# Attention and experts on one core: reciprocals through memory, bf16 parts for roots and maxima, normalisation in pieces, slots written out

## The reference, cut to what matters

```python
# x (8, 64, 128, 64), txt (8, 32, 64); all float32
h = tok(x, W)                        # patches of 16, stride 8, rfft, linear: (8, 1024, 64)
h = concatenate([h, txt], axis=1)    # (8, 1056, 64)
# layernorm(h) = (h - mean) / sqrt(var + 1e-5), over the 64 features
q, k, v = heads(layernorm(h) @ w_qkv.T)                 # 4 heads of 16
a = softmax(q @ k.T * 0.25) @ v
h = h + a.reshape(8, 1056, 64) @ w_proj.T + b_proj
n = layernorm(h)
p = softmax(n @ gate_w + gate_b)     # 8 experts, weights of the two largest kept in cw
h = h + sum_e cw[e] * (gelu(n @ W1[e] + b1[e]) @ W2[e] + b2[e])
```

## Time and profile before

| | |
|---|---|
| median of 3 runs | 997.62 us (996.91 to 1000.64) |
| the profiled execution | 1001.97 us, span 1000.2 us |
| busy in the span | PE 899.0 (90%), DVE 573.0 (57%), ACT 494.4 (49%), POOL 138.7 (14%) |
| mean granted TensorE clock | 0.922 |
| DMA | 64.58 MB in 55864 packets |

### The profile page before, as it was taken

How to read it: one execution, slowest core, us unless ns; L and a number is a source line. 1 busy time by engine, 2 the same in 40 slices (tenths; PEclk the granted TensorE clock), 3 DMA queues, 4 the chain that set the end, 5 groups by cost and what they waited for, 6 DMA issues and landing times. The chain is left out here.

```text
span 1000.2 us, 17890 instructions
## 1 busy us (share of the span) xinstructions
PE 899.0 (90%) x5900; PEld 374.9 (37%) x5900; DVE 573.0 (57%) x1201; ACT 494.4 (49%) x1189; POOL 138.7 (14%) x148
## 2 busy tenths in 40 slices
PE   5665899999999989999999999999965989899996
PEld 5241322433342343343243334333412535354443
DVE  4025565578874557876557887788230553636331
ACT  0020254466664536665446676666533454555552
POOL 0010100011010011101001101001000344444443
PEclk9965589899999988999989999999876999999998
DMA  8329351027551005536002305100006655382731
GB/s 153 57 47 163 62 62 31 3 35 119 97 69 44 2 4 67 117 67 110 2 1 30 40 2 68 44 3 1 1 5 141 120 126 117 80 184 52 155 78 22
DMA packets 55864, 64.58 MB, mean 65 GB/s; under 512 B 23893, under 2 KB 41825, under 8 KB 55777
## 3 DMA queue, kind: packets, MB, share of 16 engines
q1 hardware_dynamic: 55777, 63.46, 35.5%
HBM read 36.73 MB, written 2.43 MB: 39 GB/s over the span
## 5 line engine op out<-in xcount | busy, mean ns | idle before, releaser
L887 DVE TENSOR_REDUCE max_parts<-bank 128x1 f32<-128x512 f32 x512 | 329.6, 685 | 137.4 <-PE bank L1075 134.5
L811 ACT ACTIVATE probs<-bank 128x384 f32<-128x384 f32 (+1 forms) x768 | 313.4, 466 | 191.1 <-PE bank L1038 189.6
L1038 PE MATMUL bank<-q_stack,k_stack 99*128 99x384 bf16 (+1 forms) x768 | 229.9, 329 | 4.9 <-ACT probs L811 4.2
L1075 PE MATMUL bank<-k_stack,q_stack 96*128 96x512 bf16 x512 | 208.4, 409 | 17.2 <-DMA k_stack<-part 13.2
L1016 PE MATMUL bank<-probs,v_tiles 128*32 128x384 f32 (+1 forms) x1536 | 160.2, 490 | 5.4 <-ACT heads_out L796 5.0
L1038 PEld LDWEIGHTS bank<-q_stack,k_stack 99*128 99x128 bf16 x768 | 72.2, 99 | 196.1 <-ACT probs L811 146.1
L1285 ACT ACTIVATE hid<-bank,biases 128x352 f32<-128x352 f32 x192 | 96.0, 552 | 84.8 <-PE bank L1329 84.7
L1304 DVE SCALAR_TENSOR_TENSOR prod<-bank,biases,cwb 128x352 f32<-128x352 f32 x96 | 55.8, 582 | 120.1 <-PE bank L1317 103.0
L1329 PE MATMUL bank<-x,w 128*128 128x352 bf16 (+1 forms) x576 | 105.2, 320 | 6.3 <-DMA x<-part 6.3
L1317 PE MATMUL bank<-hid,w_sb 128*64 128x352 f32 x384 | 79.2, 491 | 7.7 <-DVE prod L1304 4.0
L1052 PE MATMUL bank<-x,tok_m 128*64 128x512 f32 x256 | 68.5, 634 | 9.4 <-DMA text_in<-in_txt 8.0
(11 more groups left out here) (146 smaller groups left out, 704.2 us busy)
## 6 DMA issues: line engine op xcount, KB each, us to landing
cwb<-gates_by_expert SPq DMA_DIRECT2D x16, 1056.0 KB, 12.1
x<-in_x SPq DMA_DIRECT2D x64, 256.0 KB, 6.9
q_stack<-part SPq DMA_DIRECT2D x48, 132.0 KB, 6.1
k_stack<-part SPq DMA_DIRECT2D x48, 132.0 KB, 6.6
x<-part SPq DMA_DIRECT2D x32, 132.0 KB, 2.5
h_res<-h_new SPq DMA_DIRECT2D x4, 528.0 KB, 3.0
h_all<-h_res SPq DMA_DIRECT2D x4, 528.0 KB, 3.1
h<-h_all SPq DMA_DIRECT2D x8, 264.0 KB, 3.2
```

The source lines that it names most:

```text
L811: nc.scalar.activation(probs[:, group % 3, h, 0:n], src, ACT.Exp, scale=SCALE).then_inc(exp_done, 1)
L887: nc.vector.tensor_reduce(max_parts[:, c, H * j + h, i % 2:i % 2 + 1], src[:, :], AX.X, ALU.max)\
L1038: last = nc.tensor.matmul(bank[:, 0:n], ks[par][0:ROWS + 3, h, P * kt:P * kt + P], qs[par][0:ROWS + 3, h, QC[qc]], start=True, stop=True)
L1075: last = nc.tensor.matmul(bank[:, :], queries(h, j), ks[par][0:ROWS, h, HALF * (i % 2):HALF * (i % 2) + HALF], start=True, stop=True)
```

## The change

- The reciprocals go from SBUF to a table in memory, `recip_rows`, and from there come back over 16 partitions per head in four transfers (`spread` 1 and 2). The three matmuls L1147 and ACT's three copies are gone; POOL multiplies at units 24, 26, 28 (`normalise`), PE projects at 27, 30, 33.
- `stack` is issued in two halves, at units 3 and 26 (7 and 30 in slot 0).
- The maxima are negated once, split into three bf16 parts on 128 partitions by DVE before the turning matmul; that matmul is bf16, and one copy on DVE ends it.
- The token variances stand at units 74, 75, 76, three tiles in each; the roots at 76 to 80, each Newton step in a unit of its own, and a split into three bf16 parts at 80 (four operations more). The spread of the roots is three bf16 matmuls for each f32 one, at units 86, 88, 90. Beside the experts the same helpers run without being spread out.
- `embed` starts two units later, `project` stands at 36, 39, 42 and 92, 94, 97.
- The loop over slots 1 to 4 is written out.

```diff
-AT_FINISH = [17, 20, 23, 26, 29, 32]
-AT_EMBED = [list(range(32, 47, 2)), list(range(48, 63, 2))]
-AT_TOKENISE = [AT_EMBED[0][-1], AT_EMBED[1][-1], 65, 68, 71, 74, 77, 80, 82, 84]
-AT_PROJECT = {"odd": [34, 37, 40], "even": [89, 92, 95]}
+AT_NORMALISE = [24, 26, 28]
+AT_FINISH = [27, 30, 33]
+AT_STACK = [3, 26]
+AT_EMBED = [list(range(34, 49, 2)), list(range(50, 65, 2))]
+AT_VARY = [74, 75, 76]
+AT_ROOT = [77, 78, 79, 80]
+AT_TOKENISE = [AT_EMBED[0][-1], AT_EMBED[1][-1], 66, 68, 70, 72, AT_VARY[-1], 86, 88, 90]
+AT_PROJECT = {"odd": [36, 39, 42], "even": [92, 94, 97]}
...
-                for i in range(2):
+                for i in range(3):
                     order.append(("spread", i, b - 1, 1 - par, q, g))
-            if u == (AT_FIRST["project"][-1] + 1 if "first" in stages else 0):
-                for i in range(2):
-                    if "following" in stages:
-                        order.append(("stack", i, b + 1, 1 - par, q + 1, g))
+            for i in range(2):
+                if "following" in stages and u == AT_STACK[i] + (AT_FIRST["project"][-1] if "first" in stages else 0):
+                    order.append(("stack", i, b + 1, 1 - par, q + 1, g))
...
-            with eng.Fori(0, 2) as q:
+            for q in range(2):
...
+        def split_roots(dve, done, n):
+            t, y = root_work[:, 1, :], roots[:, :]
+            nc.vector.tensor_copy(root_part[:, 0, :], y).then_inc(done, 1)
+            nc.vector.tensor_tensor(t, y, root_part[:, 0, :], ALU.subtract).then_inc(done, 1)
+            nc.vector.tensor_copy(root_part[:, 1, :], t).then_inc(done, 1)
+            return nc.vector.tensor_tensor(root_part[:, 2, :], t, root_part[:, 1, :], ALU.subtract)
...
-                for bp in range(2):
-                    last = nc.tensor.matmul(bank[D * bp:D * bp + D, tokens.start - WIDE * i:tokens.stop - WIDE * i],
-                                            roots[0:n, 2 * t + bp:2 * t + bp + 1].broadcast_to([n, D]),
-                                            ident[0:n, 0:n], start=True, stop=True)
+                for part in range(3):
+                    for bp in range(2):
+                        col = 2 * t + bp
+                        last = nc.tensor.matmul(bank[D * bp:D * bp + D, tokens.start - WIDE * i:tokens.stop - WIDE * i],
+                                                root_part[0:n, part, col:col + 1].broadcast_to([n, D]),
+                                                ident_half[0:n, 0:n], start=(part == 0), stop=(part == 2),
+                                                skip_group_check=True)
...
+                    elif (stage, i) == ("spread", 1):
                         sp.wait_ge(recip_done, t + 1)
-                        sp.dma_start(recip_rows[DH:P:32, :], den[:, :]).then_inc(recip_moved, 16)
+                        sp.dma_start(recip_rows, den[:, :]).then_inc(recip_moved, 16)
+                    elif stage == "spread":
+                        sp.wait_ge(recip_moved, 16 * (t + 1))
+                        for h in range(H):
+                            sp.dma_start(recip[32 * h:32 * h + DH, :], recip_rows[h:h + 1, :].broadcast_to([DH, L]))\
+                              .then_inc(recip_spread, 16)
...
-                    elif stage == "finish" and i % 2 == 0:
-                        freed(pool, i, g)
+                    elif stage == "normalise":
+                        pool.wait_ge(recip_spread, 16 * H * (t + 1))
+                        pool.wait_ge(side_free, g)
...
-                    elif stage == "finish" and i % 2 == 0:
-                        bank = full(act, i, g)
-                        nc.scalar.activation(recip[:, chunk[i // 2]], bank[:, 0:CH], ACT.Copy).then_inc(side_free, 1)
...
+                            dve.wait_ge(neg_step, step + 1)
+                            nc.vector.tensor_copy(neg_part[:, kinds, :, 0, :], negm[:, kinds, :, :]).then_inc(neg_step, 1)
+                            dve.wait_ge(neg_step, step + 2)
+                            nc.vector.tensor_tensor(neg_rest[:, kinds, :, :], negm[:, kinds, :, :],
+                                                    neg_part[:, kinds, :, 0, :], ALU.subtract).then_inc(neg_step, 1)
+                            dve.wait_ge(neg_step, step + 3)
+                            nc.vector.tensor_copy(neg_part[:, kinds, :, 1, :], neg_rest[:, kinds, :, :]).then_inc(neg_step, 1)
+                            dve.wait_ge(neg_step, step + 4)
+                            nc.vector.tensor_tensor(neg_part[:, kinds, :, 2, :], neg_rest[:, kinds, :, :],
+                                                    neg_part[:, kinds, :, 1, :], ALU.subtract).then_inc(neg_max, 1)
...
-                        nc.vector.tensor_copy(m_high[:, :], src).then_inc(shift_step, 1)
-                        stt(out=m_rest[:, :], in0=m_high[:, :], scalar=take_high, in1=src, op0=ALU.mult, op1=ALU.add)\
...
+                        nc.vector.tensor_copy(m_part[:, :], max_bank[place][0:3 * QR, 0:P]).then_inc(max_done, 1)
...
-                        last = nc.tensor.matmul(bank[0:3 * QR, 0:P], negm[:, c // 2, :, :, :].rearrange("p k n h -> p (k n h)"), ident, start=True,
-                                                stop=(c < NCH - 1), skip_group_check=True)
+                        last = nc.tensor.matmul(bank[0:3 * QR, 0:P],
+                                                neg_part[:, c // 2, :, :, :].rearrange("p k n h -> p (k n h)"),
+                                                ident_half[:, :], start=True, stop=(c < NCH - 1), skip_group_check=True)
...
-                        if i % 2 == 0:
-                            last = nc.tensor.matmul(bank[:, 0:CH], den_sel, recip_rows[:, chunk[c]], start=True, stop=True)
```

More of the change, by code:

```diff
@@ L355, in run_phase1 @@
                     side("embed", (i, j), None, None, 0, 0)
+                for j in range(2 if i == 6 else 0):
+                    side("vary", j, None, None, 0, 0)
                 side("tokenise", i, None, None, 0, 0)
+                for j in range(4 if i == 6 else 0):
+                    side("root", 1 + j, None, None, 0, 0)
             for i in range(USES["project"]):
@@ L431, in build, with token_variances @@
         wide = [slice(WIDE * i, min(WIDE * i + WIDE, L)) for i in range(NCH)]
-        def token_variances(bank, squares):
-            for t, tokens in enumerate(NORM_TILES):
+        def token_variances(bank, squares, part):
+            for t in range(3 * part, 3 * part + 3):
+                tokens = NORM_TILES[t]
                 rows = slice(0, tokens.stop - tokens.start)
@@ L438, in token_variances, with first_guess @@
             return last
-        def inverse_roots(dve, y, work, bank, done, n):
-            v, t = work[:, 0, :], work[:, 1, :]
+        def first_guess(dve, bank, done, n):
+            v, t = root_work[:, 0, :], root_work[:, 1, :]
             base = ROOT_STEPS * n
@@ L550, in norm_vector @@
                 dve.wait_ge(norm_full, NORM_FILLS * p + ROOTS + 1)
-                inverse_roots(dve, roots[:, :], root_work, norm_bank(p, ROOTS), roots2_step, p).then_inc(norm_read, 1)
+                first_guess(dve, norm_bank(p, ROOTS), roots2_step, p)
+                for k in range(3):
+                    newton_step(dve, k, roots2_step, p)
+                split_roots(dve, roots2_step, p).then_inc(norm_read, 1)
             elif name == "scale":
@@ L616, in norm_tensor @@
             elif name == "roots":
-                last = token_variances(bank, sq)
+                for part in range(3):
+                    last = token_variances(bank, sq, part)
             elif name == "scale":
-                last = spread_roots(bank, roots, i)
+                last = spread_roots(bank, i)
             elif name == "gates":
@@ L898, in side @@
                             dve.wait_ge(max_done, at + 1)
-                            for n in range(3):
-                                last = nc.vector.tensor_reduce(negm[:, c // 2, 0:nt, n, :], parts[:, 0:nt, :, :], AX.X,
-                                                               ALU.max, negate=True)
+                            step = 4 * (NCH * t + c)
+                            kinds = slice(0, 1) if c < NCH - 1 else slice(1, 3)
+                            last = nc.vector.tensor_reduce(negm[:, kinds.start, 0:nt, :], parts[:, 0:nt, :, :], AX.X,
+                                                           ALU.max, negate=True)
                             if c == NCH - 1:
@@ L1138, in side @@
                         elif i == 6:
[L1139 removed]
+                            last = token_variances(bank, sq, 2)
                         else:
[L1141 removed]
+                            last = spread_roots(bank, i - 7)
                     elif stage == "finish":
[L1143 to L1150 removed]
+                        pe.wait_ge(on_ready, NCH * t + i + 1)
+                        last = nc.tensor.matmul(bank[rows, 0:CH], projT[:, :], on[:, chunk[i]], start=True, stop=True)
```

154 lines of the change are left out of this document (80 added, 74 removed).

## The result

The changed kernel takes **995.66 us** (median of 20 executions, 984.8 to 1010.91) against 997.58 (20 executions, 995.29 to 1002.41) of the kernel before on the same chip. The ratio of the comparison is 0.9927, 95% interval 0.9905 to 0.9948; it leaves out the 7 of the changed kernel's 20 executions that lie over 1.5% above its fastest and have a mean granted clock of 0.900 to 0.912, while the means over all 20 executions of each are 997.4 and 999.0. Forecast were 978 and a range of 957 to 993.

The account below looks back on a forecast made before the run. PE was taken to bound the kernel, busy for 90% of the span. Gains of 36.9 us less 17 for the stack in halves gave -19.9 from 997.62: 978 us, range 957 to 993.

Parts of the forecast that it names:

- Term 4: Shift of the negated maxima: cheaper bf16 turning matmul, DVE's longer chain mostly covered by two units of maxima; -3.3 us.
- Terms 1 and 2: Reciprocals through memory: spreading matmuls gone from the slots, -11.6 us; shorter chain after slot 7, -5.0 us.
- Term 3: Loop's way back from slot 2 to 3: writing it out saves idle issue time and low clock, -6.6 us.
- Term 8: Stack in halves lands late in slots 1, 3, 5; ACT and PE stop at `project`, low clock follows: +17 us.
- Terms 5 to 7: In order: bf16 root fills, -3 us; variances and roots in pieces, -8; small ends beside experts and before slot 0, +0.6.
- Rival A: No wait at `project`, as the stack's second half lands before unit 36: 961 us, chance 0.20.
- rival D: Root-fill loads serialise and PE waits for the shifts: 986 to 999 us, chance 0.08.
- Rival B: Clock not given back: three low stretches stay, stalls bring their own, slot 3 falls low: 988 us, chance 0.12.
- a sum of the slots less than 10 us shorter: Sign over the slots: if their sum falls by less than 10 us, a bound other than PE has taken over.

Follow-up runs that it names:

- experiment 7: Changed kernel with both halves of the stack issued at unit 3: 1019.01 us, ratio 1.0161 to the kernel before.
- experiment 3: Kernel before with only the loop over slots 1 to 4 written out: 993.87 us, ratio 0.9926.
- experiment 11: Kernel of experiment 9 with the stack issued in two halves, at units 3 and 26: 989.06 us, ratio 0.9897.
- experiment 6: Changed kernel with odd-slot `project` at units 44, 47, 50 and the maxima in f32 as before: 973.39 us, ratio 0.9738.
- experiment 2: Changed kernel with odd-slot `project` at units 44, 47, 50 in place of 36, 39, 42: 977.89 us, ratio 0.9791.
- second run: The changed kernel, unaltered, timed and profiled again beside the kernel before: 999.0 us, ratio 0.9954.
- experiment 4: Changed kernel with the 18 variance matmuls in one burst at unit 76: 991.21 us, ratio 0.9893.
- experiment 12: Kernel of experiment 8 with the 18 variance matmuls in one burst at unit 76: 973.16 us, ratio 0.9718.
- experiment 5: Changed kernel with the negated maxima in f32 as before, DVE's four operations after the matmul: 989.93 us, ratio 0.9904.
- experiment 8: Changed kernel with f32 maxima and odd-slot `project` at units 41, 44, 51: 969.2 us, ratio 0.9674.
- experiment 9: Kernel of experiment 3 with reciprocals through memory, `embed` two units later, odd `project` at 44, 47, 50, stack in one row: 1025.24 us, ratio 1.0277.

## Why the prediction was wrong

Three steps failed. Term 4 took the longer chain on DVE as covered by two units of maxima; PE stood behind it, and -3.3 us became +5 to +8. Terms 1 and 2 were too large, -16.6 where -4.1 was measured. And the price of the clock behind every stop but the one at `project` stood at nothing. Terms 3 and 8 held, 5 to 7 brought more than forecast.

**A ledger of work and clock.** Every execution comes with its mean granted clock. Within a kernel the time follows it: over 156 executions of these kernels (all but two, of 1237 us in the kernel before and of 1906 us in that of experiment 7), 0.76 us for each 0.001, with what is left scattering by 1 to 3.5 us. So each kernel's mean can be stated at one clock, 0.925, that of the kernel before in these series. The difference of two kernels at that clock I call work and stops, the rest clock. The split is an estimate: the slopes of single kernels lie between 0.4 and 1.2, and with the changed kernel's own, 0.98, the sum below would be -13.6 and +11.7.

| kernel | mean us | mean clock | at 0.925 |
|---|---|---|---|
| before | 1000.0 | 0.925 | 1000.0 |
| loop written out (3) | 993.6 | 0.929 | 997.0 |
| + reciprocals, halves, late `project` (11) | 989.5 | 0.924 | 988.6 |
| + roots, variances, fills, even `project` at 92 (6) | 973.1 | 0.937 | 981.8 |
| + bf16 maxima (2) | 978.2 | 0.931 | 982.5 |
| + `project` at 36, the changed kernel (both series) | 998.1 | 0.913 | 989.0 |

| step of the prediction | forecast | measured | of it work, clock |
|---|---|---|---|
| term 3, loop | -6.6 | -6.4 | -3.0, -3.4 |
| terms 1 and 2, reciprocals | -16.6 | -4.1 | -8.4, +4.3 |
| terms 5, 6, 7, roots and pieces | -10.4 | -16.4 | -6.8, -9.6 |
| term 4, bf16 maxima | -3.3 | +5.1 (late) to +8.2 (early `project`) | +0.7, +4.4 to +7.5 |
| term 8, stop at `project` | +17 | +19.9 (with f32 maxima +16.8) | +6.5, +13.4 (+10.3) |
| sum | -19.9 | -1.9 | -11.0, +9.1 |

Means of six to ten executions are good to some 3 us, so no single row is better than that. The +5.1 of term 4 alone isn't clear of it, the +8.2, from 29 and 10 executions, is.

**Term 8 was right in mechanism and place.** ACT waited 4.0 to 4.5 us where I had 3, PE 2.0 to 2.5 where I had 3.8, and the clock took more than I had given it: 10 to 13 us, not 5.6. The transfers landed about 1.2 us apart, near the 1.15 of the earlier trace rows. That the total came within 3 us of the 17 is partly luck: PE's stop was too long in my sum, the clock's share too small, and the second half came late because it was issued late, not because it queued behind the first. The late place itself costs up to 1.2 us in three slots, which stands in the row above it as part of terms 1 and 2; counted to where it belongs, the stop is 3.6 us dearer and the reciprocals are 3.6 us better. Rival A, no wait, is nearest to the kernel of experiment 2: 978, and not the 961 I gave it.

**Term 3 was right**, in both halves: 2.6 of idle and 4.0 of clock were forecast, -3.0 and -3.4 measured.

**Terms 1 and 2 failed by their size, 12.5 us.** The spread matmuls did cost PE what I took them to, and after slot 7 the gain is 6.0 where 5.0 was forecast. Three things were missing. First, the first chunks are 2.3 us shorter where 1.8 was forecast, but a part of this has only moved: the third projection of `finish` moved to the second chunk, which grew by 0.8 in slot 6 (experiment 11 against 3). Slot 6, with neither stop nor `project`, gained 1.4, not 1.77; slots 2 and 4 gained 1.5 and 2.4. Second, the late `project` of that kernel, 3.6 us, which isn't the change's. Third, slot 7. I had it 1 us shorter; it is 1 us longer in experiment 11 (75.5 us against 74.4 in experiment 3), and 4 to 7 longer in the changed kernel. Of the clock, +4.3, the profile of experiment 11 shows one part, the stretch behind the 1.22 us in slot 1. The rest I can't place; it is hardly more than the means' own uncertainty.

**Term 4 had the wrong sign, and this is the step that failed most clearly.** I wrote that two units of maxima cover the chain of four more operations on DVE, and added 0.8. The matmul's price was right (0.33 to 0.14 us). The cover was not: the rows show some 0.21 us for each of the four operations, and PE stands behind them nine times, 6.1 us in all, where it was 1.8 in two places. The largest stop, 2.06 us, is in slot 7 after the last maximum, where nothing covers it (before 1.40), and the clock is low for 30.7 us of slot 7 (20.5 in the second run) where it is 13.7 before and with f32 maxima. The work so lost is about paid by the cheaper matmul (+0.7 net); the clock makes the price, +4.4 to +7.5. My rival D had this mechanism ("the shifts wait") with its 986 to 999, which holds the result. I had given it 0.08 because PE had one such wait in a slot before; but the change itself put four operations in front of that wait. That its range holds the result is in part luck: its other half, roots that serialise, didn't happen, and terms 1 and 2 and the clock made up for it.

**Terms 5 to 7 brought more than forecast, by the clock.** The fill takes 189.48 - 188.86 = 0.62 us; I had 0.63. My estimate from the Trainium skill, "TensorE: Matmul & The Clock Gate", section "LDWEIGHTS (loading the stationary operand)", 18 loads of 53 ns one after the other, would have had 0.96; the measurement decides against it. Slots 2 and 4 are 2.6 us shorter each in the kernel of experiment 6 than in that of experiment 11, which is the saving of terms 5 and 6 together, but the splitting of the burst has no share in it that experiments 4 and 12 could show. What I hadn't priced is the place where the longer chain is uncovered: before slot 0 the stop for the roots is 3.50 us where it was 2.66. I had also read both remaining waits of the earlier trace rows as lying before slot 0; one of them, 0.18 us, is in slot 7, and there the stop is now 1.48 us. The longer chain isn't shown to be its cause: with the chain of before it is 1.07 in experiment 11, and with the new one 1.05 in experiment 6. The fills also wait for `xn`: 1.47 us, or 0.85 with f32 maxima (experiments 5 and 8), where no low stretch stands before them, and less or not at all behind one. So DVE's split of the maxima has a share in this stop.

**Why the sum failed.** My forecast holds -2.8 us of clock (-4.0 in term 3, -4.4 in term 6, +5.6 in term 8) and so -17.1 of work and stops. Measured are +9.1 and -11.0. Two thirds of the miss are the clock, by this estimate: I had counted its price for the one stop that I had named, and no other. The changed kernel has stops at `project`, at the shifts, at the fills and in slot 7, and in its two profiles those that the clock fell behind were followed by 3.4 to 20.5 us at 1.2 GHz. The same program takes 984.8 us at a mean clock of 0.927 and 1010.9 at 0.900; its executions spread over 26 us, where those of the kernel before, timed beside it, lie within 7. Experiments 2, 5, 6 and 8 show that removing the stops brings most of the clock back: the mean clock is 0.913 in the changed kernel, 0.923 with the stops at the shifts cut to 2.3 us (those at `project` grow to between 2.6 and 3.0 us there), 0.931 without those at `project`, 0.937 without both, and 0.938 with the wait for the last maxima shortened too. Stops aren't the only cause: the stretch in slot 0 has none before it. Rival B had the clock as its mechanism, and its +10.3 on my -2.8 is near the +9.1, but by other stretches (the way back of the loop and the three bursts), so this is luck.

I had written that a sum of the slots less than 10 us shorter would mean that a bound other than PE has taken over. Slots 1 to 7 got no shorter, and PE still bounds them, busy for 501 of 530 us; what grew is its own stops and its time at the low clock.

## What to carry to other kernels

Where PE bounds, price every stop twice: its own length, and the stretch at half clock that may follow, which here cost as much again or more (13.4 of the 19.9 us of term 8, by the ledger). An edit that takes 0.2 us of matmul off PE and puts 0.8 us of small dependent operations in front of its next one is a loss wherever nothing is queued between them; look for the last round of the loop, where the cover is gone. When transfers on one queue become late, move what waits for them by as much (here `project` by five to nine units, 17 to 22 us), and see what stands behind them on that queue before making them one piece.

## What the runs showed of the hardware

- Within one program, time follows the mean granted clock at 0.76 us per 0.001 (156 executions of 13 programs, about 1000 us each; 0.4 to 1.2 in single programs). The length of a low stretch behind one and the same stop isn't fixed: 3.4 and 20.5 us in two profiles.
- Stops of 1.2 to 2.5 us were followed by it, but not always: behind 1.22 us the clock fell in slot 1 and stayed up in slots 3 and 5 of one profile (experiment 11), and behind 1.99 us in slot 5 of the changed kernel it stayed up. It also fell once behind three short bursts of matmuls with 2 columns each, with no stop over 0.44 us near them.
- Transfers of 132 KB issued in a row land one after the other, 1.15 us each, and three small transfers issued behind them on the same queue land after them (experiment 9).
- A store of 16.5 KB to memory and four broadcasts of it back take 739.67 - 734.17 = 5.5 us until POOL starts, against 6.5 forecast.
- Eighteen bf16 matmuls with 64 columns of weights each, in turn in two halves of the array's columns, take 0.62 us, 34 ns each.
